# Linear attention's feature map on two engines instead of three, and the class row's gates earlier in the queues

## The reference, cut to what matters

```python
q_f = jax.nn.elu(jnp.einsum('bhnd,hdf->bhnf', q, proj)) + 1.0
k_f = jax.nn.elu(jnp.einsum('bhnd,hdf->bhnf', k, proj)) + 1.0
kv = jnp.einsum('bhnf,bhnd->bhfd', k_f, v)
attn = jnp.einsum('bhnf,bhfd->bhnd', q_f, kv)
k_sum = jnp.sum(k_f, axis=2)
z = 1.0 / (jnp.einsum('bhnf,bhf->bhn', q_f, k_sum) + EPS_ATTN)
...
k_logits, k_index = jax.lax.top_k(logits, TOPK)
k_prob = jax.nn.softmax(k_logits, axis=-1)
```

## Time and profile before

| | |
|---|---|
| median of 3 runs | 775.46 us (774.49 to 777.62) |
| the profiled execution | 775.04 us, span 773.3 us |
| busy in it | TensorE 698.7, VectorE 338.9, ScalarE 294.4, GpSimd 289.1 us |
| mean granted TensorE clock | 0.948 of full speed |

### The profile page before, as it was taken

How to read it: one execution, slowest core, us unless ns; L and a number is a source line. 1 busy time by engine, 2 the same in 40 slices (tenths; PEclk the granted TensorE clock), 3 DMA queues, 4 the chain that set the end, 5 groups by cost and what they waited for, 6 DMA issues and landing times.

```text
span 773.3 us, 14754 instructions
## 1 busy us (share of the span) xinstructions
PE 698.7 (90%) x4607; PEld 614.0 (79%) x4608; DVE 338.9 (44%) x1006; ACT 294.4 (38%) x762; POOL 289.1 (37%) x324
## 2 busy tenths in 40 slices
PE   0887999999999999899999648999999999999994
PEld 0756888899887786788888547989998999999893
DVE  6576667664524544455554442232333233232320
ACT  0433655556432544345443213332323333332320
POOL 7022866666751534344440421222322222232222
PEclk9978999999679999899999859999999999999998
DMA  9515999600000891001110451221222122122210
GB/s 224 186 23 111 288 275 279 151 0 1 1 1 0 311 372 41 29 22 35 43 43 15 166 194 41 34 40 27 31 38 34 31 34 35 23 35 40 35 21 0
DMA packets 53221, 63.96 MB, mean 83 GB/s; under 512 B 6348, under 2 KB 48768, under 8 KB 53008
## 3 DMA queue, kind: packets, MB, share of 16 engines
q1 hardware_dynamic: 43616, 53.76, 24.3%
q0 software_dynamic: 8112, 9.04, 7.1%
q10 hardware_dynamic: 1456, 0.68, 0.4%
HBM read 31.01 MB, written 31.38 MB: 81 GB/s over the span
## 4 chain that ended last, share of the span: by engine, by line
PE 74%; DVE 9%; DMA 5%; issue 4%; ACT 3%; POOL 3%; SPq 1%; POOLq 0%; DVEq 0%; ACTq 0%
PE bank L1636 71%; DMA arena<-in_L_tok_Wa 2%; DMA dense<-routed_rows 1%; DMA h<-arena 1%; DVE arena L995 1%; POOL routed_rows L778 1%; ACT dense L1612 1%; POOL small L545 1%; PE bank L1814 1%; DVE small L524 1%; POOL arena L727 1%; PE bank L2146 1%; PE bank L1668 1%; DVE dense L537 1%; ACT arena L1531 1%
## 5 line engine op out<-in xcount | busy, mean ns | idle before, releaser
L1636 PE MATMUL bank<-arena,dense 128*128 (+2 forms) x1408 | 308.3, 391 | 9.0 <-ACT dense L1612 6.6
L1636 PEld LDWEIGHTS bank<-arena,dense 128*128 128x128 f32 (+1 forms) x1408 | 247.0, 193 | 49.0 <-issue 13.8
L820 POOL DMA_INDIRECT out_tokens<-dense,slot_ids x40 | 77.6, 1940 | 238.5 <-DVE dense L1358 230.7
L1612 ACT ACTIVATE dense<-bank,small 128x128 f32<-128x128 f32 x320 | 91.3, 369 | 197.6 <-PE bank L1636 197.6
L1636 PEld LDWEIGHTS bank<-dense 128*128 128x128 f32 x1280 | 150.9, 194 | 1.9
L1636 PE MATMUL bank<-dense 128*128 128x128 f32 x1280 | 151.0, 277 | 0.0
L1636 PE MATMUL bank<-dense,arena 128*128 128x256 f32 (+2 forms) x688 | 110.9, 363 | 1.0 <-ACT arena L1445 0.7
L1636 PEld LDWEIGHTS bank<-dense,arena 128*128 128x128 f32 (+2 forms) x688 | 86.3, 194 | 17.9 <-issue 4.5
L727 POOL TENSOR_TENSOR arena<-arena 128x512 f32<-128x512 f32 x64 | 80.3, 1279 | 42.0 <-ACT arena L1465 42.0
L1531 ACT ACTIVATE arena<-bank,small 128x256 f32<-128x256 f32 x128 | 53.7, 471 | 84.3 <-PE bank L1636 84.2
L1636 PE MATMUL bank<-arena 128*128 128x34 f32 (+7 forms) x756 | 81.9, 302 | 3.5 <-ACT arena L1531 1.9
(11 more groups left out here) (235 smaller groups left out, 549.5 us busy)
## 6 DMA issues: line engine op xcount, KB each, us to landing
routed_rows<-x SPq DMA_DIRECT2D x8, 2385.0 KB, 26.4
arena<-in_L_ffn_w SPq DMA_DIRECT2D x16, 1024.0 KB, 12.0
dense<-routed_rows SPq DMA_DIRECT2D x40, 132.5 KB, 2.1
arena<-in_x SPq DMA_DIRECT2D x4, 512.0 KB, 6.9
arena<-in_L_attn_w SPq DMA_DIRECT2D x2, 1024.0 KB
out_tokens<-h SPq DMA_DIRECT2D x8, 256.0 KB, 3.2
h<-arena SPq DMA_DIRECT2D x13, 128.0 KB
dense<-in_L_ffn_rw SPq DMA_DIRECT2D x1, 1024.0 KB, 9.2
```

The costliest lines, as they stand in the source:

```text
L820: pool.indirect_dma_start(out=sums[:, :], out_offset=bass.IndirectOffsetOnAxis(ap=slot_ids[par][:, 0:1], axis=0), in_=y[par], in_offset=No ...
L1612: act.activation(hT[par][:, k, :], psUP[par][c][:, P * m:P * m + P], ACT.Silu, bias=b1now[par][:, k:k + 1]).then_inc(hT_sb, 1)
L1636: return pe.matmul(out, lhsT, rhs, start=start, stop=stop, **kw)
```

## The change

ScalarE now makes both parts of the feature that need no addition: n = relu(-x) from the bank into `lin`, then exp(-n) in place in `lin`. VectorE makes the feature with one pass, max(x, 0) + `lin`, from the bank and `lin`. GpSimd has no part in it. ScalarE works in pairs of units (relu, relu, exp, exp); the copy of the turned attention rows comes after the last pair, where it stood ahead of the last unit. VectorE's features stand where the mins stood, but wait for the exp instead of the bank. TensorE writes a bank again once the sum is made (`f_sum`), not the relu. In routing step 3, ScalarE's tanh for the class row stands ahead of the turned rows of the next image instead of behind them, and TensorE's `ranks(B)` stands behind the first half of `mlp_out` instead of ahead of it. No DMA and no other instruction is changed.

```diff
--- before.py
+++ after.py
@@ -389,7 +389,6 @@
         v_sb = sem("v_sb")
         f_ps = sem("f_ps")
         f_neg = sem("f_neg")
-        f_read = sem("f_read")
         f_exp = sem("f_exp")
         f_sum = sem("f_sum")
         kv_ps = sem("kv_ps")
@@ -720,15 +719,10 @@
             residual(0, 0)
 
             def attention_step(g, par):
-                for i in range(8):
-                    u = 8 * g + i
-                    pool.wait_ge(f_exp, u + 1)
-                    dst = feature_rows(par, i)
-                    pool.tensor_tensor(dst, dst, lin[i % 4], ALU.add).then_inc(f_sum, 1)
-                    if i == 4 and (not isinstance(g, int) or g + 3 < B):
-                        root(pool, link, P, T, t_var, t_root, g + 4, t_mv[1 - par], t_rstd[1 - par])
-                    if i == 4 and isinstance(g, int) and g == B - 1:
-                        root(pool, link, P, T, x_var, x_root, 1)
+                if not isinstance(g, int) or g + 3 < B:
+                    root(pool, link, P, T, t_var, t_root, g + 4, t_mv[1 - par], t_rstd[1 - par])
+                if isinstance(g, int) and g == B - 1:
+                    root(pool, link, P, T, x_var, x_root, 1)
                 if not isinstance(g, int) or g + 1 < B:
                     residual(g + 1, 1 - par)
 
@@ -1064,12 +1058,12 @@
             def attention_step(g, par):
                 peeled = isinstance(g, int)
 
-                def negatives(i):
-                    dve.wait_ge(f_ps, 8 * g + i + 1)
-                    dve.tensor_scalar(feature_rows(par, i), psF[i % 4][:, :], 0.0, None, ALU.min
-                                      ).then_inc(f_neg, 1)
+                def features(i):
+                    dve.wait_ge(f_exp, 8 * g + i + 1)
+                    dve.scalar_tensor_tensor(out=feature_rows(par, i), in0=psF[i % 4][:, :], scalar=0.0,
+                                             in1=lin[i % 4], op0=ALU.max, op1=ALU.add).then_inc(f_sum, 1)
                 for i in range(4):
-                    negatives(i)
+                    features(i)
                 if not peeled or g >= 1:
                     attention_rows(g - 1, 1 - par, 0)
                 if not peeled or g + 2 < B:
@@ -1456,29 +1450,33 @@
             def attention_step(g, par):
                 peeled = isinstance(g, int)
 
-                def bank_out(i):
-
+                def below(i):
                     u = 8 * g + i
-                    act.wait_ge(f_neg, u + 1)
+                    act.wait_ge(f_ps, u + 1)
                     after(act, f_sum, u - 3)
-                    act.activation(lin[i % 4], psF[i % 4][:, :], ACT.Relu).then_inc(f_read, 1)
-                    act.activation(feature_rows(par, i), feature_rows(par, i), ACT.Exp).then_inc(f_exp, 1)
-                bank_out(0)
-                bank_out(1)
+                    act.activation(lin[i % 4], psF[i % 4][:, :], ACT.Relu, scale=-1.0).then_inc(f_neg, 1)
+
+                def grown(i):
+                    act.wait_ge(f_neg, 8 * g + i + 1)
+                    act.activation(lin[i % 4], lin[i % 4], ACT.Exp, scale=-1.0).then_inc(f_exp, 1)
+
+                def banks_out(i):
+                    below(i)
+                    below(i + 1)
+                    grown(i)
+                    grown(i + 1)
+                banks_out(0)
                 if not peeled or g + 1 < B:
                     q_T(g + 1, 1 - par)
-                bank_out(2)
-                bank_out(3)
+                banks_out(2)
                 if not peeled or g + 1 < B:
                     k_T(g + 1, 1 - par)
-                bank_out(4)
-                bank_out(5)
+                banks_out(4)
                 if not peeled or g + 2 < B:
                     tokens_T(g + 2, par)
-                bank_out(6)
+                banks_out(6)
                 if not peeled or g >= 1:
                     att_T(g - 1, 1 - par)
-                bank_out(7)
 
             attention_step(0, 0)
             with act.Fori(0, (B - 4) // 2) as it:
@@ -1567,10 +1565,10 @@
                 if g == 2:
                     class_part(c_mlp_ps, 1, psCT)
                 xm_T(g - 1, 1 - par)
+                if g == 3:
+                    gate_halves(B)
                 if g + 1 < B:
                     x1_T(g + 1, 1 - par)
-                if g == 3:
-                    gate_halves(B)
                 if g >= 2:
                     gate_halves(g - 2)
                 hidden(g - 1, 8 * g, ACT.Silu, rb1T, rT, IMG, range(0, 2))
@@ -1784,7 +1782,7 @@
                     for c in range(KD):
                         for i in range(4):
                             if t == 0 and c == 0:
-                                after(pe, f_read, 8 * g - 3 + i)
+                                after(pe, f_sum, 8 * g - 3 + i)
                             r0 = 2 * HD * i
                             ins = mm(psF[i][:, (t * KD + c) * P:(t * KD + c + 1) * P],
                                      kT[par][r0:r0 + 2 * HD, c, t * P:t * P + P],
@@ -1797,7 +1795,7 @@
                 for c in range(KD):
                     for i in range(4):
                         if c == 0:
-                            pe.wait_ge(f_read, 8 * g + 1 + i)
+                            pe.wait_ge(f_sum, 8 * g + 1 + i)
                         r0 = 2 * HD * i
                         ins = mm(psF[i][:, c * IMG:(c + 1) * IMG], projbd[r0:r0 + 2 * HD, c, P * i:P * i + P],
                                  qT[par][r0:r0 + 2 * HD, c, :])
@@ -2047,7 +2045,7 @@
             x1_T(0, 0)
             attend(B - 1, 1, 0)
             attend(B - 1, 1, 1)
-            pe.wait_ge(f_read, 8 * B)
+            pe.wait_ge(f_sum, 8 * B)
             pe.wait_ge(x1T_sb, 1)
             hidden(0, w1T, x1T[0], IMG, range(0, 2))
             att_T(B - 1, 1)
@@ -2088,11 +2086,11 @@
                 if g == 2:
                     class_mlp_out()
                 xm_T(g - 1, 1 - par)
-                if g == 3:
-                    ranks(B)
                 mlp_out(g, par, 0, mlp_use, range(0, 4))
                 if g == 2:
                     class_sum()
+                if g == 3:
+                    ranks(B)
                 mlp_out(g, par, 0, mlp_use, range(4, KH))
                 if g + 1 < B:
                     x1_T(g + 1, 1 - par)
```

## The result

The changed kernel took 788.54 us (median of 4 runs, 783.34 to 792.21), the kernel before beside it 776.19: a ratio of 1.0155, 95% interval 1.0093 to 1.0217. It is slower, by some 12 us, where the prediction leaned to faster and ended its range at 780.5. A second timing further down, with 9 runs, gave 783.87 us against 775.57, 1.0096 (1.0064 to 1.0128). The profiled execution took 788.51 us. A run more than 1.5% above the fastest of its kernel counts as slow here and stays out of the ratios, though not out of the medians.

A forecast was written before the change was run, and what follows sets the result against it. TensorE was taken as the bound, busy 698.7 of 773.3 us. Terms +6.0 - 1.4 + 0.5 - 0.4 - 7.1 = -2.4 us took the median 775.46 to 773.1 us, "no difference" leaning to faster; range 767.5 to 780.5.

The forecast's parts named there:

- The hole: Attention steps 1 to 6: TensorE waits for VectorE's late attention rows 0 before attend's second half; 6 x 1.0 = +6.0 us.
- The price of the new pass: VectorE's two-input feature pass, one input from PSUM, taken as 0.69 us from a row of the same shape and memories.
- the rival built on a slow pass: VectorE's new feature pass takes 1.28 us, 7.2 us more in steps 1 to 6, giving 780.3 us; chance 0.07.
- The waits of L1814: Attention steps: TensorE's four waits for ScalarE's copy of the turned tokens go; -1.4 us.
- Step 0: Attention step before 89.57 us: key-value matmuls start at 81.4 instead of 80.88 us; +0.5 us.
- Step 7: Last attention step, from 198.10 us: key-value matmuls no longer wait for GpSimd's adds, clock stays low; -0.4 us.
- the rival of a faster step 7: Last attention step holds the clock, ending in about 13.4 instead of 20.0 us, giving 766.7 us; chance 0.17.
- The gates: Class row moves in routing step 3: both TensorE waits at ranks and two clock falls go; -7.1 us.
- The clock falls oftener: Steps 1 to 6: idling before attend's narrow matmuls brings four more falls at 1.8 us, +7.2, giving 780.3 us; chance 0.15.

The follow-up runs named there:

- the first experiment: Changed kernel with VectorE's division of attention rows 0 after the second feature instead of the fourth: 765.53 us, ratio 0.9885.
- the split kernel: Changed kernel with the division after the second feature and key-value products in halves around one tile of v: 762.22 us; with the division back behind the fourth feature 793.13 us.
- the feature-only kernel: Changed kernel with the class row's two instructions in routing step 3 put back, leaving the new feature map alone: 791.59 us, ratio 1.0236.
- the sixth kernel: Changed kernel with the division after the second feature and key-value products in two halves around the whole v product of the next image: 768.86 us.

## Why the prediction was wrong

**The steps of the argument that held.** The hole: 0.89 to 0.99 us six times, 5.6 us against 6.0. The price of the new pass: 686 ns against the 0.69 us taken from L1024, so the rival built on a slow pass falls. The Trainium skill's rule of half throughput (Vector Engine (DVE) Microarchitecture Reference, "Points that are easy to get wrong") speaks of two SBUF sources; the new pass has one of its sources in PSUM, so its 686 ns neither bear the rule out nor speak against it. The waits of L1814: gone, -1.4 us. Step 0: in the first experiment, which has the same step 0, the key-value products started 8.50 us after the first key features (81.88 against 73.38) where before it was 8.01 (80.88 against 72.87), the +0.5 us forecast; TensorE waited 0.3 us for the late copy of the class row's key-value product (to 81.83), which did take the place of GpSimd's adds. (The terms given for it, 79.2, 0.82 and 1.46, add up to 81.5 and not 81.4.) Step 7: in the changed kernel's profile the key-value products started 6.99 us after the step's begin (225.17 against 218.18), no gain against the 6.93 before, where -0.4 had been forecast: the query features ended only then (222.43+2.81) and not at K+6.5. The clock fell in step 7 as before (0.58, 20.12 us for the step), so the rival of a faster step 7 did not come. The gates: -7.2 us measured alone, -7.1 forecast, and no wait left at either ranks.

**The step that failed** is a term that the sum puts at nothing: the change in the clock falls of steps 1 to 6. The hole was priced at its length alone (6 x 1.0 us), with every step at the clock it had before. The text gave the falls a rival ("The clock falls oftener"), saw the mechanism (the hole directly ahead of attend's narrow matmuls), priced it at 1.8 us a fall and four more falls, and put 0.15 on it. It is what happened, and its own sign of being wrong (a clock under 0.95 in more than two of the steps 1 to 6) came in five of them. The profiled steps 1 to 6 grew by 13.9 us. By the waits 4.2 of these are the direct term (5.6 less 1.4), and some 9.7 are clock; by the lengths of steps at full clock (18.56 against 17.70 or 17.33 us, 18.16 against 17.01) it is nearer 6 and 8. The rival had the mechanism and not the sizes: falls came in five steps, four in the second profile, against two before, which is fewer than its four more. The long one in step 1 made up for it (10 and over 13 us at the lower clock, against 3 to 3.5 for a fall at the end of the key-value products), and cost some 5 us of that step.

**Why 0.15 was wrong, as the runs show it.** The argument against the rival was that the wait behind the key-value products goes. It did go, but the clock fell at the end of those products all the same. The kernel before had falls in steps 1 and 3 and stood at 1.00 in the four others, and I read that as a state which a change of 1 us a step would leave alone. The experiments show two ways in which it was not left alone. A step that is 0.9 us longer with dense work only already lost some 4.5 us of clock (775.22 against 765.53 us, less 5.2). Idling in the same place instead of that work cost another 5 to 10 us (783.87 or 788.54 against 778.47), of which the profiles show 3.2 us in steps 1 to 6, all in step 1. And 0.35 us of hole per step cost 8.4 us in all. The late division is the cause: with one line of VectorE's queue moved the hole goes, and the kernel is 18 to 23 us faster; in the split kernel the same line is worth 27 to 31 us.

**What stays open.** How the lost clock divides between the idling and the length of the step is not settled: each kernel has one or two profiles, and the single falls change from execution to execution. Nor is it shown why the clock falls at the end of the key-value products in one step and not in the next. Whether the low clock of step 0 in the first profile of the changed kernel (0.68) has to do with the change isn't settled: the second profile and the feature-only kernel have 0.89 and 0.90 in nearly the same stretch, and the start of step 1 lies anywhere from 88.3 to 95.8 us in the profiles of these kernels.

## What to carry to other kernels

When work moves to an engine that has a queue of its own, look at what stands behind it in that queue and who waits for it. Here four passes that wait for ScalarE stood ahead of a division that TensorE waits for, and moving that division up by two places turned a loss of 1 to 1.5% into a gain of 1.2%. And a wait on TensorE's path is not always worth its own length: ahead of narrow matmuls it cost three to four times that here, most of it through the clock, while 0.68 us ahead of wide ones in the sixth kernel brought no fall. In a kernel whose profile already shows the lower clock in some steps, the number of falls is a term of the sum and not a constant of it.

## What the runs showed that was not expected

- The same microsecond costs different amounts: 0.35 us of waiting per step cost 8.4 us in all (773.9 against 765.5), 0.9 us of dense matmuls per step 9.7 us (775.2), and 0.95 us of waiting 18 to 23 us.
- Dense work put in the hole paid for itself: two matmuls per step whose result nobody reads took the changed kernel from 783.9 or 788.5 to 778.5 us, though the profile still has four falls.
- Breaking an unbroken run of narrow matmuls with 1 us of dense ones held the clock at 1.00 in all profiled steps 1 to 6 when no hole was there, and the runs, but for one, lay within 1.5 us (761.76 to 763.22). The sixth kernel, with 2 us of dense ones, held it in all profiled steps too. With the hole it did nothing for the time (793.1 us).
- A scalar_tensor_tensor of 128x512 with one input in PSUM and one in SBUF takes 686 ns, the time of a two-input pass, as the mean of all 64.
